# A graph-network kernel's edge passes: 16 instead of 18 of the 28 edge columns of a group taken from TensorE's one-hot products, 12 instead of 10 from gathers

## The reference, cut to what matters

```python
def _L0_gnn_ref(x, edge_weight, src, dst):            # narrow pass 0
    m = jnp.tanh(x[src] * edge_weight[:, None])
    return jax.ops.segment_sum(m, dst, num_segments=x.shape[0])
...
# L2, narrow pass 1
msg = inputs[src] * timestamp
h = jax.ops.segment_max(msg, dst, num_segments=inputs.shape[0])
return h @ W.T + b
...
# L3, narrow passes 2 and 3
agg = jax.ops.segment_sum(x[src], dst, num_segments=n_nodes)
h = (1.0 + eps) * x + agg
h = jax.nn.relu(h @ wa + ba) @ wb + bb
...
x = _layernorm(x + _L0_gnn_ref(x, edge_weight, src, dst), axis=-1)
```

## Time and profile before

| | |
|---|---|
| median of 3 runs | 8206.96 us (8204.55 to 8208.66) |
| the profiled execution's own time | 8196.03 us |
| its span | 8194.2 us |
| mean granted TensorE clock | 0.959 of full speed |
| busy: TensorE matmul, VectorE, ScalarE, GpSimd | 7100.0, 6989.1, 1570.8, 5336.9 us |
| instructions | 205237 |

### The profile page before, as it was taken

One profiled execution on the slowest core, in us unless ns is written; L12 is line 12 of the kernel. 1 busy time (PEld: TensorE's weight loads), 2 busy tenths in 40 slices (PEclk: granted clock), 3 DMA queues, 4 the chain that ended last, 5 costly groups with the idle time before them and its releaser, 6 DMA issues.

```text
span 8194.2 us, 205237 instructions
## 1 busy us (share of the span) xinstructions
PE 7100.0 (87%) x77871; PEld 6660.7 (81%) x77871; DVE 6989.1 (85%) x12224; ACT 1570.8 (19%) x3861; POOL 5336.9 (65%) x4570
## 2 busy tenths in 40 slices
PE   5999985888888988888887099999499997799994
PEld 5999975777777777777776099999499997799994
DVE  7999976999999999999999488888488886688884
ACT  0000002444444444444443200000000000000000
POOL 3555557888888888888886655555455555455554
PEclk9999998999999999999999599999799998899997
DMA  2222213555555455455554211111111111111110
GB/s 88 87 83 87 87 48 91 152 155 155 152 155 156 152 156 154 152 156 155 152 155 145 77 48 46 47 48 46 29 48 48 48 48 32 42 48 47 47 48 21
DMA packets 738221, 757.27 MB, mean 92 GB/s; under 512 B 153760, under 2 KB 698336, under 8 KB 738112
## 3 DMA queue, kind: packets, MB, share of 16 engines
q1 hardware_dynamic: 592640, 667.34, 24.7%
q0 software_dynamic: 140528, 86.77, 6.7%
q10 hardware_dynamic: 5008, 2.59, 0.1%
HBM read 239.80 MB, written 519.73 MB: 93 GB/s over the span
## 4 chain that ended last, share of the span: by engine, by line
PE 41%; DVE 30%; issue 23%; POOL 4%; DMA 1%; DVEq 1%; ACT 0%; ACTq 0%; POOLq 0%; SPq 0%; another core or an unknown queue 0%
PE ps L798 41%; DVE amax_room L1206 6%; DVE spare L1211 4%; DVE flat L1233 3%; DVE msg L1111 2%; DVE stt L928 2%; POOL got L451 2%; DVE flat L928 2%; DVE run L1132 1%; DVE spare L1215 1%; DVE raw L928 1%; DVE wide_buf L928 1%; DVE flat L1090 1%; DVE junk L1138 1%; POOL wide_buf L451 1%
## 5 line engine op out<-in xcount | busy, mean ns | idle before, releaser
L451 POOL DMA_INDIRECT msg<-feat,cidx x1680 | 1686.0, 1004 | 1580.9 <-PE ps L798 1172.2
L798 PE MATMUL ps<-parts,wide_buf 128*128 128x160 bf16 x30240 | 2123.2, 233 | 291.1 <-DVE wide_buf L1090 279.7
L798 PEld LDWEIGHTS ps<-parts,wide_buf 128*128 128x128 bf16 x30240 | 2100.2, 98 | 303.8 <-issue 283.7
L451 POOL DMA_INDIRECT hsrc<-feat,aidx x1568 | 1897.0, 1210 | 457.8 <-issue 327.8
L798 PE MATMUL ps<-parts,flat 128*128 128x160 bf16 x30240 | 2113.3, 233 | 25.7 <-DVE flat L1090 21.1
L798 PEld LDWEIGHTS ps<-parts,flat 128*128 128x128 bf16 x30240 | 2093.6, 98 | 33.1 <-DVE flat L1090 25.1
L845 PEld LDWEIGHTS ps<-wsb,zT 102*128 102x128 f32 x9408 | 1464.1, 190 | 222.9 <-ACT zT L684 201.2
L845 PE MATMUL ps<-wsb,zT 102*128 102x192 f32 (+1 forms) x9408 | 1543.3, 313 | 101.9 <-ACT zT L684 101.2
L1111 DVE TENSOR_REDUCE msg<-raw 128x288 f32<-128x2880 f32 x224 | 1130.4, 5046 | 7.8
L928 DVE TENSOR_TENSOR raw<-ps,amask 128x960 f32<-128x960 f32 x448 | 737.9, 1657 | 463.4 <-PE ps L798 351.0
L451 POOL DMA_INDIRECT msg<-in_x,cidx x560 | 561.3, 1002 | 553.5 <-PE ps L798 310.0
(11 more groups left out here) (218 smaller groups left out, 4681.3 us busy)
## 6 DMA issues: line engine op xcount, KB each, us to landing
state_tab<-flat SPq DMA_DIRECT2D x784, 512.0 KB
raw<-quot_tab SPq DMA_DIRECT2D x224, 576.0 KB
run_tab<-run SPq DMA_DIRECT2D x224, 224.0 KB
top_tab<-spare SPq DMA_DIRECT2D x392, 128.0 KB
msg<-feat,cidx POOLq DMA_INDIRECT x1680
hsrc<-feat,aidx POOLq DMA_INDIRECT x1568
efs<-in_ef SPq DMA_DIRECT2D x392, 34.0 KB
msg<-in_x,cidx POOLq DMA_INDIRECT x560
```

Of the source, the lines that this page charges most:

```text
L451: return pool.indirect_dma_start(dest, None, table, rows_at(idx))
L798: last = nc.tensor.matmul(block.rearrange("p (q c) -> p q c", c=D), hot[s][:, m, t * P:(t + 1) * P], parts[:, m * Q:(m + 1) * Q, part, :], ...
```

## The change

R goes from 18 to 16, so A = U - R goes from 10 to 12. TensorE has 240 matmuls a group instead of 270 and counts twelve steps instead of ten. Each one-hot tile has 16 x 128 columns instead of 18 x 128. Ten columns instead of twelve lie in the shared banks: three banks with three blocks and the last with one, so VectorE reads them with two multiplications, one of nine columns (RW - OWN) and one of one column. The reduction is over 16 columns. POOL issues twelve gathers a group. The two large rooms `wide_buf` and `flat` are sized by the attention's nodes (7168 elements) instead of by 7 * R * P / 2 (8064).

```diff
--- before.py
+++ after.py
@@ -22,7 +22,7 @@
 P = 128
 N, E, D = 6250, 200000, 16
 U = 28
-R = 18
+R = 16
 OWN = 6
 A = U - R
 G = 4
@@ -46,8 +46,10 @@
 QW = Q * D
 DW = DC * D
 NCH = NB // DC
+ROOM = 4 * DC * DD
 PB = 4
 CB = 3
+RW = OWN + (R - OWN) // CB * CB
 F = D + 1
 FROM = (0, 6, 10)
 NEW = (0, 6, 12, D)
@@ -58,7 +60,7 @@
 assert NB % 2 == 1 and SL < NG // 2 and NB % DC == 0 and K % (2 * G) == 0 and NG % 2 == 0 and 2 * G == 8
 CONT, BOTH, CONT_NEG, BOTH_NEG = range(4)
 
-assert MB * (Q - 1) < NB <= MB * Q and CB * QW <= 512 and OWN == 2 * CB and R - OWN == 4 * CB and K % DW == 0
+assert MB * (Q - 1) < NB <= MB * Q and CB * QW <= 512 and OWN == 2 * CB and R - OWN <= 4 * CB and K % DW == 0
 
 FP = mybir.dt.float32
 BF = mybir.dt.bfloat16
@@ -162,7 +164,7 @@
         wsb = sb("wsb", [P, 3, CF * 2 * D])
         aring = sb("aring", [P, 2, 2, G])
         raw = sb("raw", [P, R * P + R * QW])
-        wide_buf = sb("wide_buf", [P, 7 * R * P // 2])
+        wide_buf = sb("wide_buf", [P, ROOM])
         amax_room = sb("amax_room", [P, 2 * DC * DD])
         amax = amax_room[:, 0:2 * G * DD].rearrange("p (a g c) -> p a g c", a=2, g=G)
         spare = sb("spare", [P, (DC - 1) * DD])
@@ -171,7 +173,7 @@
         vT = spare[:, 0:NCH * P].rearrange("p (c q) -> p c q", q=P)
         diag = spare[:, NCH * P:(NCH + 3) * P].rearrange("p (a q) -> p a q", q=P)
         wts = z_room[:, 0:K]
-        flat = sb("flat", [P, 7 * R * P // 2])
+        flat = sb("flat", [P, ROOM])
         st = flat[:, 0:2 * G * TW].rearrange("p (a g c) -> p a g c", a=2, g=G)
         ebuf = wide_buf[:, 2 * DD:2 * DD + 2 * G * TW].rearrange("p (a g c) -> p a g c", a=2, g=G)
         fixw = wide_buf[:, 0:2 * DD].rearrange("p (t c) -> p t c", t=2)
@@ -1104,8 +1106,12 @@
                     tt(picked_rows(0, OWN), mine_banks[s].rearrange("p b (r c) -> p b r c", c=D), mask_rows(0, OWN),
                        ALU.mult).then_inc(q["read"][s], 1)
                     dve.wait_ge(q["pick"][s], (done + j + 1) * A)
-                    tt(picked_rows(OWN, R), shared.rearrange("p b (r c) -> p b r c", c=D), mask_rows(OWN, R),
-                       ALU.mult).then_inc(s_share, 1)
+                    last = tt(picked_rows(OWN, RW), shared[:, 0:(RW - OWN) // CB].rearrange("p b (r c) -> p b r c", c=D), mask_rows(OWN, RW),
+                              ALU.mult)
+                    if RW < R:
+                        last = tt(picked[:, RW:R], shared[:, (RW - OWN) // CB, 0:(R - RW) * QW].rearrange("p (r q c) -> p r q c", q=Q, c=D),
+                                  amask[:, RW:R].unsqueeze(3).to_broadcast([P, R - RW, Q, D]), ALU.mult)
+                    last.then_inc(s_share, 1)
                     dve.wait_ge(s_share, n * NG + 2 * j + s + 1)
                     dve.wait_ge(q["read"][s], done + j + 1)
                     hold(v.tensor_reduce(msg[:, s, A:U, :], picked.rearrange("p r q c -> p r c q"), AX.X, ALU.add))
```

## The result

The changed kernel takes 8553.45 us (median of 4 runs, 8541.03 to 8557.72) against 8205.75 us for the kernel before in the same runs (8202.72 to 8208.66): a ratio of 1.0421 [1.0403, 1.0439]. It is 348 us slower, where 419 us faster was forecast. Of the two it is the sign that has to be explained.

A forecast was written before the change was run, and what follows sets the result against it. TensorE was taken to bound passes 1 to 3 and pass 0's last 5 groups, VectorE pass 0's other 51. Savings of 349 + 10 + 56 + 4 = 419 us from 8207 gave 7788 us, range 7765 to about 7820, or 7830 with small lags.

The forecast's parts named there:

- I cost the gathers at nothing: POOL's twelve gathers a group: a late one stays within VectorE's cover of 6.5 us, so 0 us was charged.
- ahead of them, where the forecast would have looked for it: Passes 1 to 3: TensorE idle ahead of its groups was named as a sign that the forecast is wrong.
- TensorE's 2.08 us a group: 30 matmuls fewer at 69.4 ns: 349 us over 168 groups of passes 1 to 3, 10 us in pass 0.
- VectorE's 1.10 us: Smaller reduction, products, one-hots and mask save this per group, bounds 0.75 and 1.3; 56 us over 51 groups of pass 0.
- POOL's fit: Twelve gathers take 16.1 us against TensorE's 16.65 in pass 1, and 17.4 against 18.66 in pass 0.
- (a): POOL becomes the bound because VectorE's one-hots keep it from working: 8157 us; chance 3 in 100.
- 1.09 us allowed: Sign on POOL: a mean gather above this, 12 x 1.39 us with the gap, would prove the forecast wrong.
- (b): POOL's gather waits are handled one after another, 1.92 us each: some 830 us slower, 9040 us; chance 2 in 100.
- the 1.56 from which it decides: POOL's us a gather, 18.7 / 12, from which the rival of gather waits handled one after another decides.
- the 1.25 us behind a stop: Interval between two POOL gathers, one waiting, in the trace of before; taken as the shortest pace, under the 1.39 us counts.
- (c): VectorE saves far less because instruction cost is mostly fixed: 7864 us with 0 saved; chance 6 in 100, in-between cases included.
- (d): POOL is just short at 1.45 us a gather, 17.4 us a group, losing 126 us: 7914 us; chance 7 in 100.

The follow-up runs named there:

- slow chips: Chips 3, 4 and 6 and the place of the first result; the changed kernel took 8556.62, 8552.58, 8471.76 and 8553.45 us there.
- unpaced: POOL's waits for TensorE's counts removed: from the changed kernel, 7756.05 us (chip 9), 10765.13 (chip 4); from the kernel before, 8181.93 (chip 9), 10187.22 (chip 6).
- even: A group's first gather also waits for a TensorE count, chip 1: changed kernel 7758.79 us, kernel before 8180.48, R = 17 7970.47.
- in pairs: Changed kernel where only gathers 2, 4, 6, 8 and 10 of a group wait for TensorE's counts: 8705.86 us, 1.0606 of the kernel before (chip 3).
- the lead: Changed kernel where gather u > 3 waits for count u - 3 instead of u: 9081.56 us, 1.1064 of the kernel before (chip 3).
- the first set: Four kernels on chip 9, without the changed kernel: R = 16 without gather waits 7756.05 us or with ten gathers 7755.99; R = 18 without waits 8181.93, with twelve gathers 8181.44.

## Why the prediction was wrong

**The step that failed** is "I cost the gathers at nothing". The text asked whether POOL has the time for twelve gathers, and what a late one would cost VectorE. It never asked what gathers close together do to TensorE, which doesn't wait for them at all. On the slow chips that is the largest term of the sum. The idle came inside the groups, not ahead of them, where the forecast would have looked for it. Lengths of a group, from the first and the last matmul of pass 2 or 3 over 56 groups (read from the trace's records), in us:

| | TensorE's work alone | on chips 9, 1 | on the slow chips |
|---|---|---|---|
| 270 matmuls, 10 gathers (before) | 18.7 | 18.7 (unpaced; even) | 18.8 |
| 270 matmuls, 12 gathers | 18.7 | 18.7 | 20.3 |
| 255 matmuls, 11 gathers | 17.7 | 17.7 (even) | 19.1 to 19.2 |
| 240 matmuls, 10 gathers | 16.65 | 16.6 | 17.3 to 17.4 |
| 240 matmuls, 12 gathers (the change) | 16.65 | 16.65 | 19.9 to 20.3 |
| 240 matmuls, 12 gathers, unpaced | 16.65 | 16.6 | 29.7 |

In the right column a group with twelve paced gathers takes nearly the same whether TensorE has 240 or 270 matmuls (on chip 6 19.9 and 20.3 us), 1.66 to 1.69 us a gather. The loss in the first result is 20.26 (the mean of passes 1 to 3) - 16.65 = 3.6 us in each of 168 groups, 605 us. In pass 0 the groups take 21.65 us there and 18.40 on chip 1: 56 x 3.25 = 182. Together 787 us, and the two times of the changed kernel, 8553 and 7760, are 793 apart.

**How it feeds itself.** Counts each 1.39 us leave POOL, which can do 1.25, only 0.14 us to catch up with for each gather. After any stop POOL is behind, and its next gathers come 1.25 us apart. In the changed kernel's first trace a matmul takes 3 to 7 ns more than its 69 (from its start to the next one's, inside a group) while no or one gather in a row has come within 1.4 us of the one before, 12 ns more with two, 83 with three and 94 with four; over the trace of chip 1 the same count gives 2 ns at the most. In such a hold-up POOL stands still too, so POOL is behind again. By the records of passes 1 to 3, a waiting gather starts 2.7 us (median) after the start of the matmul that makes its count, where in the kernel before it was 1.0. With a count each 1.87 us, as before, POOL regains its place within a few gathers, and the hold-ups come to 4 to 8 us in a pass instead of 184 to 233. That rows of gathers hold TensorE up is shown by the unpaced kernels, in pairs and with the lead; that it feeds itself fits the traces but was not tested apart.

**The terms that held.** On chips 9 and 1, where gathers do cost nothing, the sum was right: 419 us forecast, 420 measured (chip 1). TensorE's 2.08 us a group, VectorE's 1.10 us (pass 0's 56 groups went from a mean of 19.65 us, with 270 matmuls on chip 9, to 18.40 on chip 1, 1.25 less where (51 x 1.10 + 10) / 56 = 1.18 was forecast) and POOL's fit all stand. The forecast of 7788 was made against 8207, so the same sum against 8181 would have been 7762.

**The rivals.** (a) is out: gathers took 977 ns on the mean against 1.09 us allowed. The Trainium skill ("SBUF — State Buffer", section "Who interferes with whom") has VectorE's 2-port operations and GpSimd block each other fully. The traces show less: a gather that lies wholly inside the one-hots takes 1.18 us on the mean in the kernel before (0.94 to 1.58) and 1.11 in the changed one (0.94 to 1.85), against 0.96 and 0.95 clear of them. The same section says, in its talk of the ports, that TensorE never waits on anyone. No run here shows a port; what the changed kernel's trace shows is a TensorE that stands still for up to 1.2 us by "issue" while gathers are in work.

(b) had the right side and the right engine: 1.69 us a gather is beyond the 1.56 from which it decides. Its mechanism is wrong. The gathers aren't handled one after another at 1.92 us; they go mostly in rows of three or four at 1.25 us, the next one comes 2.4 to 2.9 us after the last of them, and without any wait it gets worse. I had given it 2 in 100, on the 1.25 us behind a stop of the earlier trace rows. Those lines show one interval between two gathers, and TensorE wasn't in the view.

(c) and (d) are out: VectorE saved what was reckoned, and POOL alone is fast enough.

**What could have been seen.** In the kernel before, the same thing stands in the view of waits, as the 15.1 us in 41 places shown above. By the records, its matmuls take 44 ns more than usual where three gathers in a row have come within 1.4 us of the one before (151 matmuls). It was small, so I let it go; a change that makes such places the rule deserved a look at what TensorE does beside them.

**What stays open.** Why one chip, or one set, shows the hold-up and another does not; and what it is on TensorE's side. The view names no wait for data or buffers: the idle lies inside a group, and both weight loads and matmuls stop. The gathers' transfers aren't slower where TensorE is held up: the packets of 512 bytes in their queue take 38 ns (median) in the changed kernel's first trace and 41 on chip 1. Nor was the issuing of a gather by POOL told apart from its transfer: each variant changed both at once. POOL's own semaphore step after each wait isn't needed for the hold-up, since the unpaced kernels have neither wait nor step; whether one gather for two columns would help wasn't tried. Whether an even pace with R = 17 beats the kernel before on chips 3, 4 and 6 is open too, since that set ran on chip 1. Of the kernels here that compute everything, the kernel before is the fastest on those chips and the changed one, in any pacing that was tried, on chips 9 and 1.

## What to carry to other kernels

Work that is moved to an idle engine isn't free because that engine has the time: ask what its instructions do to the others when they come close together, and look at the bounding engine beside the densest such rows that the trace of before already has. When a change cuts the interval at which one engine paces another, compare it with the follower's shortest pace, since what is left between them is all it can catch up with (0.62 us a gather before, 0.14 after). And put the kernel to be explained beside its variants each time: in the first set two kernels seemed to cure what wasn't ill there.

## What the runs showed of the hardware

- The same kernel of one core took 8553 us in the first result, 8557, 8553 and 8472 on chips 3, 4 and 6, and 7760 on chip 1, each time with runs that agree within 0.3%. The kernel before told the two kinds apart by little: 8196 to 8211 us against 8180.5. Without pacing the changed kernel differs by 39%: 7756 and 10765.
- Rows of indirect gathers 1.25 us apart slow TensorE on the slow chips to a few matmuls each 0.7 or 1.4 us (chip 4, unpaced), mostly from a row's fourth gather on (83 ns more a matmul in the first trace, against 12 from the third). VectorE isn't touched: its reduction took 4472 ns there and 4488 on chip 1.
- Where TensorE stood still often, its granted clock was lower: 0.83 of full speed over the unpaced kernel on chip 4, a mean of stretches at 2.4 and 1.2 GHz, against 0.955 on chip 9.
